# A transformer block on one core: single passes of five engines' queues put in another order

## What is computed

```python
q = softmax(x @ Wq.T + bq, over the 16 channels of a head)
k = softmax(x @ Wk.T + bk, over the tokens)
state = einsum('bhnd,bhne->bhde', k, v)       # v = x @ Wv.T + bv
out = einsum('bhnd,bhde->bhne', q, state)
x = layernorm(x + (ln(out) @ Wo.T + bo))
h = gelu(layer_norm(x) @ ternary(w1).T + b1)
x = layernorm(x + layer_norm(h) @ ternary(w2).T + b2)
```

## Time and profile before

| | us |
|---|---|
| median of 3 runs | 552.31 (552.25 to 552.56) |
| the profiled execution's own time | 551.79 |
| its span in the profile | 549.9 |
| TensorE busy | 532.1 |
| VectorE busy | 481.8 |
| ScalarE busy | 478.6 |
| GpSimd busy | 414.7 |

### The profile page before, as it was taken

The page is one execution under the profiler, slowest core; times in us unless marked ns, Lnnn a source line. Parts: engine busy times, 40 slices in busy tenths (PEclk is TensorE's granted clock), DMA queues, the critical chain, the costliest instruction groups (busy, mean ns, idle before and its releaser), DMA issues.

```text
span 549.9 us, 10913 instructions
## 1 busy us (share of the span) xinstructions
PE 532.1 (97%) x3541; PEld 492.0 (89%) x3541; DVE 481.8 (88%) x1227; ACT 478.6 (87%) x952; POOL 414.7 (75%) x429
## 2 busy tenths in 40 slices
PE   8999999999999999989999999999999999999993
PEld 7999999898999989879987999999999999999992
DVE  5888998989899898878788899999999999999896
ACT  5745789798978878778799999999999999999996
POOL 2965969877796986478468878888888877776782
PEclk9999999999999999999999999999999999999997
DMA  8530050320705021070011003322125253010012
GB/s 337 203 122 1 1 230 2 131 100 11 297 1 229 2 87 69 1 266 5 0 40 41 1 0 117 117 76 79 50 68 116 78 93 94 34 53 38 39 40 114
DMA packets 12679, 46.51 MB, mean 85 GB/s; under 512 B 1360, under 2 KB 3792, under 8 KB 10448
## 3 DMA queue, kind: packets, MB, share of 16 engines
q1 hardware_dynamic: 12336, 45.28, 23.7%
q10 hardware_dynamic: 288, 0.54, 0.3%
HBM read 29.01 MB, written 16.81 MB: 83 GB/s over the span
## 4 chain that ended last, share of the span: by engine, by line
PE 68%; ACT 11%; DVE 11%; POOL 5%; issue 3%; DMA 2%; SPq 0%; POOLq 0%; DVEq 0%; ACTq 0%
PE ring L2005 19%; PE qps_sps_aps_then_y L2027 19%; PE qps_sps_aps_then_y L1787 5%; PE qps_sps_aps_then_y L1893 5%; PE qps_sps_aps_then_y L1873 5%; PE ring L1815 5%; DVE z L1285 3%; PE ring L1945 2%; POOL xt_lo L462 2%; PE ring L1920 1%; PE ring L1908 1%; PE ring L1960 1%; ACT ek L745 1%; DMA xc<-in_x_first_dram 1%; POOL ff_accp_over_xt_lo L588 1%
## 5 line engine op out<-in xcount | busy, mean ns | idle before, releaser
L2027 PE MATMUL qps_sps_aps_then_y<-ff_w_over_xc_lo,ff_a_lo_over_qw 128*128 128x258 f32 x512 | 126.5, 283 | 0.0
L2027 PE MATMUL qps_sps_aps_then_y<-ff_w_over_xc_lo,ff_a_hi_over_xc_lo 128*128 128x258 f32 x512 | 126.4, 283 | 0.0
L1367 DVE SCALAR_TENSOR_TENSOR ff_a_lo_over_qw<-ring,ff_rho,ff_a_hi_over_xc_lo 128x512 fp32r<-128x512 f32 x128 | 92.8, 743 | 12.5 <-ACT ff_a_hi_over_xc_lo L881 11.4
L2005 PE MATMUL ring<-ff_ht_hi_over_qw,t 128*128 128x512 f32 x256 | 103.7, 405 | 0.1
L2005 PE MATMUL ring<-ff_ht_lo_over_xc_hi,t 128*128 128x512 f32 x256 | 100.5, 393 | 0.0
L2027 PEld LDWEIGHTS qps_sps_aps_then_y<-ff_w_over_xc_lo,ff_a_lo_over_qw 128*128 128x128 f32 x512 | 96.8, 189 | 3.3
L2027 PEld LDWEIGHTS qps_sps_aps_then_y<-ff_w_over_xc_lo,ff_a_hi_over_xc_lo 128*128 128x128 f32 x512 | 96.7, 189 | 3.4
L863 ACT ACTIVATE ring<-ring,bias 128x512 f32<-128x512 f32 x128 | 84.5, 689 | 6.7 <-PE ring L2005 5.5
L588 POOL TENSOR_TENSOR ff_accp_over_xt_lo<-ff_accp_over_xt_lo,ff_sq_over_ek_et_hi 128x512 f32<-128x512 f32 x66 | 86.0, 1303 | 2.0
L879 ACT ACTIVATE ff_sq_over_ek_et_hi<-ring 128x512 f32<-128x512 f32 x128 | 80.5, 629 | 0.5
L881 ACT CAST ff_a_hi_over_xc_lo<-ring 128x512 fp32r<-128x512 f32 x128 | 79.5, 621 | 0.0
(11 more groups left out here) (200 smaller groups left out, 1615.4 us busy)
## 6 DMA issues: line engine op xcount, KB each, us to landing
xt<-in_x_tok_dram SPq DMA_DIRECT2D x8, 1024.0 KB, 4.8
out_dram<-ff_z_over_et_lo SPq DMA_DIRECT2D x15, 512.0 KB, 2.7
x_scratch<-z SPq DMA_DIRECT2D x14, 514.0 KB, 3.6
ff_x_over_w_raw_xc<-x_scratch SPq DMA_DIRECT2D x14, 514.0 KB, 5.1
xc<-in_x_chan_dram SPq DMA_DIRECT2D x6, 1024.0 KB, 6.9
w_raw<-in_w_dram SPq DMA_DIRECT2D x2, 1024.0 KB, 5.4
ek<-in_x_chan_dram SPq DMA_DIRECT2D x1, 1024.0 KB, 8.2
x_scratch<-xt SPq DMA_DIRECT2D x2, 512.0 KB, 7.9
```

Of the source, the lines that this page charges most:

```text
L1367: nc.vector.scalar_tensor_tensor(out=ff_a_lo[:, m % DEPTH], in0=ff_bank(k, m), scalar=ff_rho[:, m:m + 1], in1=ff_a_hi[:, m % DEPTH].bitcas ...
L2005: mm = nc.tensor.matmul(ff_bank(k, m), t1[:, c, m * P:(m + 1) * P], h[:, k % 2, c], start=(c == 0 and j == 0), stop=(c == CH - 1 and j == 1))
L2027: last = nc.tensor.matmul(ff_yps[:, t, 0:C + 2], a[:, m % DEPTH, t * P:(t + 1) * P], ff_w2[:, m], start=(m == 0 and j == 0), stop=(m == FC ...
```

## The change

Six places, all of them order; no instruction is added or removed, and no semaphore's count.

```diff
 GpSimd, attention loop (b = 1 to 6)
                 chan_lo(b + 2, 1)
-                tok_c(b, 1)
-                attention_rstd(b - 1, 1)
                 if b in (2, 5):
+                    attention_rstd(b - 1, 1)
+                    tok_c(b, 1)
                     ternary_round(b // 5, 2)
+                else:
+                    tok_c(b, 1)
+                    attention_rstd(b - 1, 1)
 GpSimd, batch 7
             norm_rstd(NB - 3, 0)
-            norm_rstd(NB - 3, 1)
             q_normalise(NB - 1, 0)
             q_normalise(NB - 1, 1)
+            norm_rstd(NB - 3, 1)
             tok_lo(NB - 1, 0)
...
             attention_rstd(NB - 1, 1)
-            norm_rstd(NB - 1, 0)
             ff_square_sum(0, 2)
             ff_square_sum(0, 3)
             ff_square_sum(0, 4)
             ff_square_sum(0, 5)
+            norm_rstd(NB - 1, 0)
             ff_norm_rstd(3)
 ScalarE, attention loop
                 et_high(b, 0)
                 if b in (3, 6):
-                    ternary_out(b // 6, 0)
+                    product_out(b - 1, 5)
                 et_high(b, 1)
                 if b in (3, 6):
-                    ternary_out(b // 6, 1)
-                product_out(b - 1, 5)
+                    ternary_out(b // 6, 0)
+                else:
+                    product_out(b - 1, 5)
                 pt_high(b, 2)
                 pt_high(b, 3)
+                if b in (3, 6):
+                    ternary_out(b // 6, 1)
                 et_high(b, 2)
 ScalarE, batch 7
             squares(NB - 3, 1)
+            projected_high(NB - 2)
             k_exponent(NB - 1, 0)
-            projected_high(NB - 2)
             normalise(NB - 3, 0)
             k_exponent(NB - 1, 1)
             product_out(NB - 2, 0)
+            product_out(NB - 2, 1)
             tok_hi(NB - 1)
-            product_out(NB - 2, 1)
             product_out(NB - 2, 2)
 TensorE, attention loop, and the same in batch 7
                 e_transposes(b, 1)
+                q_transposes(b, 3)
                 attend(b - 1, 7)
-                q_transposes(b, 3)
                 state_sum(b, 0)
```

More of the change, by code:

```diff
@@ L2106, in _ @@
             e_transposes(NB - 1, 1)
+            q_transposes(NB - 1, 3)
             attend(NB - 2, 7)
-            q_transposes(NB - 1, 3)
             state_sum(NB - 1, 0)
```

## The result

The changed kernel takes **556.96 us** (median of 4 runs, 555.75 to 557.4) where the kernel before, measured beside it, takes 552.28 (4 runs, 551.65 to 552.56). The ratio is 1.0081, with a 95% interval of 1.0069 to 1.0093: slower by 4.7 us. Predicted were 554.3 us and a range that ended at 555.2. The sign is right, the size is less than half of it. The profiled execution took 557.28 us, with a span of 555.4 us and a mean granted clock of 0.993.

A forecast was written before the change was run, and what follows sets the result against it. The prediction took TensorE, busy for 532.1 of 549.9 us, as the bound. Its terms, 0.70 + 0.95 - 1.52 + 2.1 - 0.25, gave +2.0 us, so a median of 554.3 us, range 551.2 to 555.2.

The forecast's parts named there:

- The step that failed: Handover: squared sums, freed of norm_rstd(7,0), end some 3 us sooner; TensorE's wait for ff_a_lo goes, about 1.1 us.
- the hold: Residual z passes, batch 7's r_lo: a VectorE pass lasts as long as GpSimd's large pass beside it; one z pass 2.62 us.
- The term: Handover, norm_rstd(7,0) behind the four squared sums: -0.25 us left because ScalarE is full there; bounds 0 and -1.1.
- TensorE's order, +0.70: Query transposes ahead of attend 7: pt_lo late, +0.35 us each in batches 1 and 4, +0.70 in all.
- Rival 2: Query transposes ahead of attend 7 cost nothing, pt_lo arriving in time; same speed, 552.0 us; chance 0.14.
- The swap in batches 2 and 5, +0.95: attention_rstd ahead of tok_c: a later z pass is held; +0.3 us in batch 2, +0.65 in batch 5.
- The copy ahead of the ternary passes, -1.52: Batches 3 and 6: state sum stops waiting for ScalarE's copy, pt_lo is late next; -0.76 us each, -1.52 in all.
- Batch 7, +2.1: Last attention batch, three edits: r_lo held beside qw, xt_hi's cast 2.15 us late behind the copy; +2.1 us.
- Rival 1: z passes of batches 2 and 5 and r_lo of batch 7 are not held: faster, 551.1 us; chance 0.16.
- Rival 3: Only r_lo of batch 7 escapes, the z passes are held: +0.7 us, 553.0 us; chance 0.12.

The follow-up runs named there:

- experiment 1: Kernel before with only the handover's edit, norm_rstd(7,0) behind the four squared sums: 554.75 us, ratio 1.0049.
- experiment 10: Kernel before with the handover's edit plus a wait that starts the squared sums after VectorE's last residual pass of batch 7: 552.07 us, ratio 1.0006.
- experiment 11: Changed kernel plus a wait that starts the four squared sums after VectorE's last residual pass of batch 7: 554.28 us, ratio 1.0037.
- experiment 12: The kernel of experiment 2 run once more, unaltered, for a second profile: 555.74 us.
- experiment 3: Kernel before with only TensorE's last query transposes of a batch put ahead of attend 7: 551.68 us, ratio 0.9991.
- experiment 6: Kernel before with only attention_rstd put ahead of tok_c in batches 2 and 5: 551.56 us, ratio 0.999.
- experiment 5: Kernel before with only the product copy of batches 3 and 6 ahead of the two ternary passes, run again for its profile: 551.23 us.
- experiment 7: Kernel before with only both qw passes of batch 7 put ahead of norm_rstd(5,1): 553.14 us, ratio 1.0022.
- experiment 8: Changed kernel with batch 7's cast of xt_hi back ahead of the second product copy of batch 6: 555.08 us, ratio 1.0059.
- experiment 13: Kernel before with batches 3/6 copy, batches 2/5 swap, and in batch 7 r_hi's cast earlier, norm_rstd(5,1) between qw passes, ff_norm_rstd(0) between xt_lo passes: 550.36 us.
- experiment 2: Changed kernel with the handover as before, norm_rstd(7,0) back ahead of the squared sums: 555.0 us, ratio 1.005.
- experiment 9: Changed kernel with only the second qw pass of batch 7 back behind norm_rstd(5,1): 554.94 us, ratio 1.0056.

## Why the prediction was wrong, step by step

- **The step that failed** is this one: "The sums end some 3 us sooner and this wait goes, about 1.1 us." It went wrong twice. First, it counted the 2.9 us of `norm_rstd`'s own instructions and not the 3.07 us that the first of them waits for ScalarE, with the sums behind it. Freed of both, the sums ended at 288.66 us in experiment 1 instead of 294.21, 5.5 us sooner, and started at 282.23 instead of 288.37, just where VectorE's `znm` and `ff_xn` passes stand. Second, it never asked what they would now run beside. The prediction had used the hold for the `z` passes and for `r_lo`, both with two operands in SBUF. `ff_xn` and `znm` read one, and they were held as well: 0.35 us to 1.39 for the longest `ff_xn` pass, 0.17 to 1.32 for `znm`. A residual pass, with two operands, was held too (0.48 us to 1.06), so even the hold as the prediction knew it spoke against the term. The term was -0.25 and measured +2.1 (experiments 1, 10 and 11); its bounds, 0 and -1.1, left no room for a loss. The old wait did go, and gave 1.1 us, as it said. By the Trainium skill, page "SBUF — State Buffer", section "SBUF: two separate sides", a VectorE instruction is shut out by a GpSimd one in two cases, with two SBUF inputs or in a performance mode that uses two ports; the prediction took up the first alone. The trace shows that the first case alone is too narrow: `ff_xn` and `znm` have one SBUF input and are held. Whether they run in a mode of the second case, no run here shows. Not every pass with one SBUF input is held (rows in the last section).
- **A term that was missing** is the clock. In the profiled execution TensorE ran at 1.2 GHz for 3.4 us behind the handover's wait. There it cost less than the 1.6 us of experiment 12: the handover lost 2.72 us with the fall and 2.13 without it (experiment 1), since a later wait shrinks in exchange. The profiled execution is so made up of 0.46 (start-up), 2.28 (attention), 2.13 (hold) and some 0.6 (clock, by the difference of two executions): 5.5 us over the 551.79 of before, 557.28. The two middle terms alone give 4.4 of the 4.7 us between the medians. Of the other three runs the longest, 557.4, has a mean clock of 0.992, under all profiles without a fall; the other two have 0.994, which leaves it open.
- **TensorE's order, +0.70**: the local price was right (+0.39 against +0.35), the place where it ends was not. By itself the edit costs nothing (experiment 3). With the swap of batches 2 and 5 the chain behind `r_f` takes the lag in as well. Rival 2, that this order is free, was right on this term, for another reason than it gave: `pt_lo` was late, but a later wait swallowed it.
- **The swap in batches 2 and 5, +0.95**: the held pass moved as worked out, with the same 2.62 us, but what it adds was mostly TensorE's lag over again. By itself it gains 0.4 us (experiment 6). In the changed kernel this item and TensorE's order come to 0.36 by batch 3 and 0.43 + 0.34 in batches 4 and 5, 1.13 together, where the sum had 1.65. Alone, TensorE's order had made the waits for `r_f` vanish; with the swap they stay at 0.5 us each, since the chain behind `r_f` comes later too. The two items meet in one wait and do not add.
- **The copy ahead of the ternary passes, -1.52**: right on the spot, -0.74 and -0.67. Missing was the 0.36 us given back in batch 4, where `r_lo` now meets a `qw` pass (experiment 5). A gain is a shift as well, and can move a pass into a hold. With it the item is -1.05 in the changed kernel and -0.95 alone.
- **Batch 7, +2.1**: right in sum (2.2), in the held `r_lo` (2.47 us; "over 2 us" was predicted), in the query transposes that stay where they were, and in the wait for `et_lo` (2.18). These are the rows:

```profile
239.68 1.95 POOL L483 TENSOR_TENSOR qw<-qw,qinv 128x1024 f32<-128x1024 f32 x1 [0.95 <-DVE qinv L1192]
...
239.97 2.47 DVE L1150 TENSOR_TENSOR r_lo<-r_f,r_hi 128x768 fp32r<-128x768 f32 x1
...
242.49 0.45 PE L1879 MATMUL qps_sps_aps_then_y<-r_hi,pt_hi 128*128 128x384 f32 x1 [1.63 <-DVE r_lo L1150]
...
246.52 1.92 ACT L731 CAST xt_hi<-xt 128x2048 fp32r<-128x2048 f32 x1
...
254.50 0.62 DVE L1358 TENSOR_SCALAR ff_xn<-ff_x_over_w_raw_xc,ff_rs 128x256 f32<-128x256 f32 x2 [3.36 <-POOL ff_rs L540]
...
256.11 0.38 PE L1899 MATMUL qps_sps_aps_then_y<-et_hi,xt_hi 128*128 128x256 f32 x1 [2.18 <-DVE et_lo L1150]
```

  Its split was wrong: half is the copy, half is the hold by way of `kbias` and `k_exponent` (experiments 7 and 8). One list of everything queued behind `r_lo` on VectorE would have shown it.
- **Rivals 1 and 3**, in which holds do not bite, are refuted by the rows of `r_lo`, 1.6 us in batch 4 and 2.47 in batch 7.

## What to carry to other kernels

When a pass of GpSimd is freed from a wait, look at which VectorE passes it will now run beside, before counting what comes sooner: here four sums that ended 5.5 us sooner cost 2.1 us of the kernel's time, and one wait put ahead of them took it all back. The wait that was removed had been keeping two engines apart. Count how far a freed pass moves by the waits it stood behind, not only by the work. Put GpSimd's large passes beside VectorE work that reads PSUM (`ff_a_lo` took its 0.75 us beside the sums) or beside its idle time, and count for a held pass all that is queued behind it. A lag ahead of a later wait of its own size was free here (experiment 3), so a price is only known once it is followed to the next wait; and a wait that is new and long can cost more than itself, through TensorE's clock.

## What the runs showed of the hardware

- Some VectorE passes with a single SBUF operand are held by a large GpSimd pass over SBUF: `ff_xn` (128x256) took 2.25 us beside a 2.40 us `xt_lo` pass, 0.35 alone; even `znm`, 128x4, took 1.32 us beside a 1.3 us sum, 0.17 alone. Both are TENSOR_SCALAR passes from SBUF to SBUF.
- Others are not held. In the changed kernel a reduction and a reciprocal of one SBUF tensor run inside the first GpSimd pass below, and a 128x1 TENSOR_SCALAR inside the second:

```profile
15.73 2.42 POOL L452 TENSOR_TENSOR xc_lo<-ek,xc_hi 128x1024 fp32r<-128x1024 f32 x1
15.78 1.21 DVE L1185 TENSOR_REDUCE qsum<-qw 128x64 f32<-128x1024 f32 x1
17.02 0.55 DVE L1192 RECIPROCAL qinv<-qsum 128x64 f32<-128x64 f32 x1
...
18.22 1.94 POOL L483 TENSOR_TENSOR qw<-qw,qinv 128x1024 f32<-128x1024 f32 x1
18.68 0.21 DVE L1231 TENSOR_SCALAR kbm<-kmx,vecs 128x1 f32<-128x1 f32 x1
```

  They end before the pass beside them does, and `qinv` takes the same 0.55 us as in the earlier trace rows. Where the line runs between the two kinds, no run here shows.
- The hold goes by whole GpSimd passes and not by the size of the held one: `r_lo` (0.95 us alone) ended 0.81 to 0.82 us behind the `qw` pass beside it in all four rows of it shown here, however long it had been held, and `ff_xn` of experiment 13 ended 0.15 us behind `xt_lo`. In the handover each sum held one VectorE pass, and the two `ff_xn` passes that had begun just before a sum took their usual 0.34 us.
- TensorE's granted clock was 0.50 for 3.41 us behind a wait of 1.6 to 2.2 us, in one execution of experiment 2's kernel and not in the other (555.74 and 553.89 us). It cost 1.6 us there, as much again as the wait, 1.3 us in experiment 9 and some 0.6 in the changed kernel. In eight profiles with a wait of 1.6 us or more it came three times. No profile in which TensorE's waits stayed at or under 1.3 us showed it between 10 us and TensorE's last matmul.
